# The head of a fused three-layer kernel rewritten: tile loads, moments, weights and 1/sqrt moved between engines

## The reference

```python
x = x + 0.5 * ffn(layernorm(x))
x = x + attn(layernorm(x))        # rope, causal softmax, projection by Wo, bias
x = x + 0.5 * ffn(layernorm(x))
# ffn(h): scores against 128 slots, the 8 highest chosen, softmax over them, their values
# through two small matrices; times a gate; plus h
# gate: sigmoid of a clipped sum of a learned term (gelu MLP) and
#       log1p(var(h)) / mean(log1p(var(h))), the mean over all 2048 rows
# layernorm(x) = (x - mean) / sqrt(var + 1e-5)
```

## Time and profile before

| | us |
|---|---|
| median of three runs | 1456.96 |
| lowest and highest | 1456.8, 1458.84 |
| the profiled execution | 1457.93 |
| its span, first to last instruction | 1456.1 |

### The profile page before, as it was taken

How to read it: one execution, slowest core, us unless ns; L and a number is a source line. 1 busy time by engine, 2 the same in 40 slices (tenths; PEclk the granted TensorE clock), 3 DMA queues, 4 the chain that set the end, 5 groups by cost and what they waited for, 6 DMA issues and landing times.

```text
span 1456.1 us, 26905 instructions
## 1 busy us (share of the span) xinstructions
PE 1370.9 (94%) x8689; PEld 777.2 (53%) x8818; DVE 1137.5 (78%) x2816; ACT 958.9 (66%) x2423; POOL 848.0 (58%) x1343
## 2 busy tenths in 40 slices
PE   5578999998999999999999999999999999999986
PEld 4344555554555655555555655555555555555543
DVE  6787868887788878979778787888777788868655
ACT  4567686776677767666766766666766667666734
POOL 3778778888875454446656455445644565454412
PEclk9799999999999999999999999999999999999998
DMA  9646668778667566556657666557666677555443
GB/s 314 224 90 145 144 154 196 174 178 203 164 157 150 126 142 133 130 123 149 141 129 158 134 125 142 125 129 145 138 139 133 133 151 157 121 142 108 93 76 116
DMA packets 440269, 212.16 MB, mean 146 GB/s; under 512 B 382113, under 2 KB 383329, under 8 KB 440129
## 3 DMA queue, kind: packets, MB, share of 16 engines
q1 hardware_dynamic: 438016, 206.24, 61.5%
q10 hardware_dynamic: 2112, 4.19, 0.9%
HBM read 91.88 MB, written 25.17 MB: 80 GB/s over the span
## 4 chain that ended last, share of the span: by engine, by line
PE 71%; POOL 12%; ACT 7%; DVE 6%; issue 3%; DMA 1%; SPq 0%; DVEq 0%; ACTq 0%
PE PJ L1235 16%; PE PJ L1234 15%; PE PJ L1236 15%; POOL t L562 4%; PE PV L1234 4%; PE PV L1236 4%; PE PV L1235 4%; PE SC L1399 4%; PE SC L1400 4%; PE SC L1398 3%; ACT p L727 2%; POOL wsp L554 2%; POOL qTl L567 2%; POOL wosp L554 1%; POOL oTl L577 1%
## 5 line engine op out<-in xcount | busy, mean ns | idle before, releaser
L577 POOL TENSOR_TENSOR oTl<-of,oTf 128x256 f16<-128x256 f32 x256 | 167.6, 675 | 375.5 <-ACT oTf L719 375.5
L727 ACT ACTIVATE p<-p,mn 128x512 f32<-128x512 f32 (+3 forms) x512 | 280.9, 549 | 86.3 <-DVE mn L1041 86.1
L1051 DVE SCALAR_TENSOR_TENSOR phl<-p,ri,phl 128x128 f16<-128x128 f32 (+3 forms) x512 | 311.1, 647 | 0.0
L562 POOL TENSOR_TENSOR t<-t 128x256 f32<-128x256 f32 x320 | 232.8, 749 | 43.0 <-DVE t L1014 42.4
L738 ACT ACTIVATE phl<-p,ri 128x128 f16<-128x128 f32 (+3 forms) x512 | 245.6, 550 | 4.1
L1234 PE MATMUL PJ<-XT,wsp 128*128 128x512 f16 x640 | 243.4, 380 | 5.0 <-DVE t L1014 3.3
L1235 PE MATMUL PJ<-XT,wsp 128*128 128x512 f16 x640 | 243.1, 380 | 0.0
L1236 PE MATMUL PJ<-XT,wsp 128*128 128x512 f16 x640 | 243.1, 380 | 0.0
L567 POOL TENSOR_TENSOR qTl<-t,qTh 128x256 f16<-128x256 f32 x256 | 169.7, 684 | 93.2 <-ACT qTh L703 93.2
L1041 DVE CUSTOM_DVE_ANT_0 p<-SC,maskw 128x512 f32<-128x512 f32 (+3 forms) x512 | 219.7, 485 | 2.1
L1235 PE MATMUL PJ<-wosp,oTf 128*128 128x512 f16 x512 | 194.0, 379 | 4.4
(11 more groups left out here) (208 smaller groups left out, 2679.1 us busy)
## 6 DMA issues: line engine op xcount, KB each, us to landing
wsp<-kept SPq DMA_DIRECT2D x150, 256.0 KB, 3.1
wosp<-kept SPq DMA_DIRECT2D x96, 256.0 KB, 3.4
raw<-in_wqkv SPq DMA_DIRECT2D x48, 256.0 KB, 4.4
kept<-wsp SPq DMA_DIRECT2D x42, 256.0 KB, 2.5
raw<-in_wo SPq DMA_DIRECT2D x32, 256.0 KB, 4.7
kept<-wosp SPq DMA_DIRECT2D x32, 256.0 KB, 3.1
X<-in_x ACTq DMA_DIRECT2D x4, 1024.0 KB, 11.4
pTf<-phl SPq DMA_TRANSPOSE x256, 3.8
```

Of the source, the lines that this page charges most:

```text
L562: ins = nc.gpsimd.tensor_tensor(t1[:, j, c], t1[:, j, c], t2[:, j, c], ALU.add)
L727: ins = nc.scalar.activation(pt, pt, ACT.Exp, bias=mn[:, par, i:i + 1], scale=-1.0, accum_out=rs[:, par, i:i + 1])
L1051: nc.vector.scalar_tensor_tensor(out=phl[:, par, low(i, 0):low(i, i) + 1, :], in0=p[:, par, SOFF[i]:SOFF[i] + w].rearrange("p (k t) -> p k ...
```

## The change

- Loads. ScalarE's queue issues X's tiles 0, 1 and 2, 3 as two loads, then three small ones (`lrb`, `bu1`, `wu2T`); tiles 4 to 15 are issued by SP, between its other loads. SP no longer waits for tiles 8 to 11 before the weights.
- Moments. VectorE keeps tiles 0 to 9; for tiles 10 to 15 ScalarE sums the differences to the row's first element and their squares (`sums`), and VectorE turns the sums into moments. In the second normalisation the sum comes with the update of `X` (`aux_first`) and the squares from ScalarE (`squares`).
- 1/sqrt. `root` is now Ln and then Exp with scale -0.5, which are in one table set; `ve`, `sd` and the reciprocal go. `gelu` loads its table ahead of its wait and the other set right after.
- GpSimd makes the first base updates of `X` (`x * xa + xb`), the low half `ul`, and both halves of the first four weights. A weight's low half goes in two pieces of 256 columns in place of four of 128, in the loop too.
- The four `W` weights of n = 1 leave the head's list and are made in steps 6 to 8, as for later n.
- V of n = 0 is projected ahead of K, its first three row tiles before K and the last after Q. VectorE does the whole rope of K and the first Q but for the cast. The second `deviation` of k = 0 moves from the head into step 0.
- `penalty` and `minima_ffn` go; `top` marks and takes the minimum for its two tiles with one fused operation per tile, in the loop and the tail too.
- On TensorE the four key matmuls of the setup come first, and `HID` ahead of the `PV` product.

The diff, cut; of the head's written-out lists only the lines that stay or are new are shown, their old form is in the kernel printed above. Three dots also part pieces of different functions.

```diff
+BYACT = 10
+NSPLIT = 4
...
-FIRST = [("K", 0, 0, 0), ("Q", 0, 0, 0), ("V", 0, 0, 0), ("Q", 0, 1, 0)]
+FIRST = [("V", 0, 0, 0), ("K", 0, 0, 0), ("Q", 0, 0, 0), ("Q", 0, 1, 0)]
...
-  + [(1, k) for k in KINDS])
+  + [(1, k) for k in PIECES])
...
+load_x(4, 4)
...
+load_x(8, 4)
+load_x(12, 4)
+for dst, src in ((bu2[:, :], f_bu2.to_broadcast([P, 1])), (gw[:, :], f_gw.to_broadcast([P, 1])),
...
-sp.wait_ge(ld_x[2], 16)
...
+    if r < NSPLIT:
+        pool.wait_ge(ld_r[r], 16)
+        nc.gpsimd.tensor_copy(w[:, 0, :].bitcast(BF16), raw[:, r, :]).then_inc(w_own, 1)
+        pool.wait_ge(w_own, r + 1)
+    else:
+        pool.wait_ge(w_hi, r - NSPLIT + 1)
+    for c in parts(2):
...
-for r in range(6):
+pool.wait_ge(ld_fu, 16)
+pool.wait_ge(fs_hi, 5)
+nc.gpsimd.tensor_tensor(ul[:, :, :], fwu1T, uh[:, :, :], ALU.subtract).then_inc(fs_ul, 1)
+pool.wait_ge(x_ab[0], 1)
+for n in range(4):
+    nc.gpsimd.tensor_scalar(X[:, n, :], X[:, n, :], xa[:, 0, n:n + 1], xb[:, 0, n:n + 1], ALU.mult,
+                            ALU.add).then_inc(x_up[0], 1)
+for r in range(NHEAD):
     weight_low(r)
-penalty(0, 0)
-for r in range(6, NHEAD):
-    weight_low(r)
-for kind, n, idx, _ in FIRST:
-    if kind in "QK":
-        rope(kind, n, idx)
+rope("Q", 0, 1)
...
-for i in range(4):
-    act.dma_start(X[:, 4 * i:4 * i + 4, :], x_v[:, 4 * i:4 * i + 4, :]).then_inc(ld_x[i], 16)
+roots, totals = [0], [0]
+for n in (0, 2):
+    act.dma_start(X[:, n:n + 2, :], x_v[:, n:n + 2, :]).then_inc(ld_x[n], 16)
+for dst, src in ((lrb[:, :], f_lr.to_broadcast([P, NSLOT])), (bu1[:, :], f_bu1), (wu2T[:, :], f_wu2T)):
+    act.dma_start(dst, src).then_inc(ld_fs, 16)
+LOGS = "natural_log_exp_and_others"
...
-    act.wait_ge(ln_v[k], call + 1)
-    nc.scalar.activation(sd[:, k, c0:c1], ve[:, k, c0:c1], ACT.Sqrt).then_inc(ln_sd[k], 1)
+    c = slice(c0, c1)
+    act.wait_ge(ln_v[k], 3 if k == 0 and call else call + 1)
+    nc.scalar.activation(lvar[:, k, c], mv[:, k, c, 1], ACT.Ln, bias=eps[:, 0:1]).then_inc(ln_log, 1)
+    roots[0] += 1
+    act.wait_ge(ln_log, roots[0])
+    nc.scalar.activation(rstd[:, k, c], lvar[:, k, c], ACT.Exp, scale=-0.5).then_inc(ln_sd[k], 1)
...
+def gelu(f, bb, loaded=False):
+    if not loaded:
+        nc.scalar.preload_act_table(ACT.Gelu_apprx_tanh)
...
+    nc.scalar.preload_act_table_set(LOGS)
...
+def total(n, func, sums_):
+    j = totals[0]
+    totals[0] += 1
+    if j >= NROPE:
+        act.wait_ge(a_tot, j - NROPE + 1)
+    nc.scalar.activation(t2[:, j % NROPE, :], X[:, n, :], func, bias=X[:, n, 0:1], scale=-1.0,
+                         accum_out=sums_).then_inc(a_tot, 1)
+def sums(n):
+    act.wait_ge(ld_x[n // 4 * 4], 16)
+    total(n, ACT.Identity, s1[:, 0, n:n + 1])
+    total(n, ACT.Square, s2[:, 0, n:n + 1])
...
+nc.scalar.preload_act_table_set(LOGS)
+act.wait_ge(cst0, 1)
+act.wait_ge(fs_pe, 1)
+nc.scalar.copy(rk[:, :], PJ[0:RDIM, 3, 0:NSLOT]).then_inc(fs_ev, 1)
+act.wait_ge(fs_pe, 2)
+nc.scalar.copy(rmat[:, :], PJ[0:BOT, 2, 0:NSLOT]).then_inc(fs_ev, 1)
+root(0, 0, 0, 4)
 for c in range(CC):
     act.wait_ge(fs_pe, 3 + c)
     nc.scalar.copy(ah[:, c, :], setup_bank(c)).then_inc(fs_hi, 1)
 act.wait_ge(ld_fu, 16)
 nc.scalar.copy(uh[:, :, :], fwu1T).then_inc(fs_hi, 1)
 for i in range(4):
     turned_hi(0, 0, i)
+nc.scalar.preload_act_table(ACT.Gelu_apprx_tanh)
+for n in range(BYACT, BYACT + 2):
+    sums(n)
+act.wait_ge(fs_pe, 7)
+nc.scalar.copy(u1T[:, :], SC[0:VB, 0, 0:NSLOT]).then_inc(fs_ev, 1)
+for n in range(BYACT + 2, NT):
+    sums(n)
+act.wait_ge(ld_fs, 96)
+gelu(0, 0, True)
+exps_ffn(0, 0)
+gate_exp(0, 0, 4)
+logs(0)
 act.wait_ge(fs_pe, 8)
 nc.scalar.copy(v2h[:, :], PV[:, :]).then_inc(fs_hi, 1)
 e_hi(0, 0)
 gate_exp(1, 0, 4)
 for i in range(4):
+    squares(i)
+root(1, 0, 0, 4)
+root(0, 1, 4, NT)
+for r in range(4, 7):
     weight_high(r)
+turned_hi(1, 0, 0)
+turned_hi(1, 0, 1)
+weight_high(7)
+turned_hi(1, 0, 2)
+turned_hi(1, 0, 3)
+for r in range(8, NHEAD):
+    weight_high(r)
+rope("K", 0, 0)
+rope("Q", 0, 0)
+value_hi(0)
+rope("Q", 0, 1)
...
-    link(nc.vector.reciprocal(rstd[:, k, c], sd[:, k, c]))
     link(nc.vector.tensor_tensor(nw[:, k, c], rstd[:, k, c], rstd[:, k, c], ALU.mult))
-    link(nc.vector.tensor_tensor(nw[:, k, c], nw[:, k, c], ve[:, k, c], ALU.mult))
+    link(nc.vector.scalar_tensor_tensor(out=nw[:, k, c], in0=var, scalar=EPS, in1=nw[:, k, c],
+                                        op0=ALU.add, op1=ALU.mult))
...
-    if j == 1:
-        nc.vector.tensor_scalar(mr[:, :, :], mr[:, :, :], 0.99 * SELECTED, MASKED,
-                                ALU.is_gt, ALU.mult).then_inc(r_pen[f], 1)
+    ts = slice(2 * j, 2 * j + 2)
+    link(nc.vector.tensor_scalar(mr[:, ts, :], mr[:, ts, :], 0.99 * SELECTED, MASKED, ALU.is_gt, ALU.mult))
+    for i in (2 * j, 2 * j + 1):
+        n = 4 * bb + i
+        ins = nc.vector.tensor_tensor_reduce(
+            out=asc[:, f, i, :], in0=asc[:, f, i, :], in1=mr[:, i, :], scale=1.0, scalar=3e38,
+            op0=ALU.add, op1=ALU.min, accum_out=mnr[:, f, n:n + 1])
+    ins.then_inc(r_mn[f], 1)
...
+def rope_total(r):
+    dve.wait_ge(rope_mul, r + 1)
+    nc.vector.tensor_tensor(t1[:, r, :], t1[:, r, :], t2[:, r, :], ALU.add).then_inc(rope_sum, 1)
+def rope_low(r, hi, lo):
+    dve.wait_ge(rope_hi, r + 1)
+    nc.vector.tensor_tensor(lo, t1[:, r, :], hi, ALU.subtract).then_inc(rope_lo, 1)
...
+def moments_of_sums():
+    c = slice(BYACT, NT)
+    dve.wait_ge(a_tot, 2 * (NT - BYACT))
+    link(nc.vector.tensor_scalar(s1[:, 0, c], s1[:, 0, c], 1.0 / C, None, ALU.mult))
+    nc.vector.tensor_tensor(mv[:, 0, c, 0], X[:, c, 0], s1[:, 0, c], ALU.subtract)
+    link(nc.vector.tensor_tensor(dm[:, 0, c], s1[:, 0, c], s1[:, 0, c], ALU.mult))
+    nc.vector.scalar_tensor_tensor(out=mv[:, 0, c, 1], in0=s2[:, 0, c], scalar=1.0 / C, in1=dm[:, 0, c],
+                                   op0=ALU.mult, op1=ALU.subtract).then_inc(ln_v[0], 1)
+def aux_first(i):
+    dve.wait_ge(r_aux[0], i + 1)
+    dve.wait_ge(x_up[0], i + 1)
+    dve.wait_ge(r_gs[0], 1)
+    nc.vector.scalar_tensor_tensor(out=X[:, i, :], in0=bank(("AUX", 0, 0, i)), scalar=gs[:, 0, i:i + 1],
+                                   in1=X[:, i, :], op0=ALU.mult, op1=ALU.add,
+                                   accum_out=s1[:, 1, i:i + 1]).then_inc(r_xd[0], 1)
+def variance_of_squares():
+    c = slice(0, 4)
+    dve.wait_ge(r_xd[0], 4)
+    link(nc.vector.tensor_scalar(mv[:, 1, c, 0], s1[:, 1, c], 1.0 / C, None, ALU.mult))
+    link(nc.vector.tensor_tensor(dm[:, 1, c], X[:, c, 0], mv[:, 1, c, 0], ALU.subtract))
+    link(nc.vector.tensor_tensor(dm[:, 1, c], dm[:, 1, c], dm[:, 1, c], ALU.mult))
+    dve.wait_ge(a_tot, 2 * (NT - BYACT) + 4)
+    nc.vector.scalar_tensor_tensor(out=mv[:, 1, c, 1], in0=s2[:, 1, c], scalar=1.0 / C, in1=dm[:, 1, c],
+                                   op0=ALU.mult, op1=ALU.subtract).then_inc(ln_v[1], 1)
...
 for n in range(4):
     arrived(n)
 variance(0, 0, 4)
 deviation(0, 0, 0, 4)
 for i in range(4):
     normal(0, 0, i)
+for c in range(CC):
+    setup_lo(c)
 for i in range(4):
     turned_lo(0, 0, i)
+base_factors(0, 0, 4)
+for n in range(4, 8):
+    arrived(n)
 dve.wait_ge(ld_fs, 96)
 take_scores(0, 0, 0)
 top(0, 0, 0)
+for n in range(8, BYACT):
+    arrived(n)
 take_scores(0, 0, 1)
 top(0, 0, 1)
 learned(0, 0)
 gate_1(0, 0, 4, 1)
+variance(0, 4, BYACT)
+moments_of_sums()
+dve.wait_ge(ln_v[0], 3)
+variance_logs(0)
+log_sum(0)
 dve.wait_ge(fs_hi, 6)
 nc.vector.tensor_tensor(v2l[:, :], PV[:, :], v2h[:, :], ALU.subtract).then_inc(fs_lo, 1)
 e_lo(0, 0)
 log_mean(0)
 gate_2(0, 0, 0, 4)
 gate_3(0, 1, 0, 4)
 scales(0, 0, 4, 1)
 for i in range(4):
+    aux_first(i)
+variance_of_squares()
...
+rope("K", 0, 0)
+rope_total(0)
+rope("Q", 0, 0)
+rope_total(1)
+rope_low(0, kTh[:, 0, :], kTl[:, 0, :])
+rope_low(1, qTh[:, 0, :], qTl[:, 0, :])
+value_lo(0)
+rope("Q", 0, 1)
...
+    if s == 0:
+        deviation(0, 1, 4, NT)
+        base_factors(0, 4, NT)
...
+pe.wait_ge(ld_fq, 16)
+for c in range(CC):
+    mm(setup_bank(c)[:, NSLOT:2 * NSLOT], fwq[:, c * P:(c + 1) * P], fkeyT[:, :], start=True, stop=True)
...
+pe.wait_ge(fs_ul, 1)
+ffn_task(HEAD[6])
 pe.wait_ge(fs_ev, 3)
 mm(PV[:, :], u1T[:, :], fwvuT, start=True, stop=True).then_inc(fs_pe, 1)
-pe.wait_ge(fs_lo, 5)
...
+project_values(0, range(TB - 1))
+project("K", 0, 0)
+project("Q", 0, 0)
+project_values(0, range(TB - 1, TB)).then_inc(s_v, 1)
+project("Q", 0, 1)
```

171 lines of the change are left out of this document (48 added, 123 removed).

## The result

| us | before | after |
|---|---|---|
| median | 1457.03 (4 runs) | 1446.76 (4 runs) |
| lowest and highest | 1456.8, 1458.84 | 1445.04, 1448.45 |
| the profiled execution | 1457.93 | 1448.45 |
| its span | 1456.1 | 1446.6 |

The ratio is 0.9926, with a 95% interval of 0.9914 to 0.9938: 10.3 us faster, where 23 were forecast, and 1.8 above the upper end of the range. In what follows L12 is line 12 of the kernel that the row is from.

What follows compares the result with a forecast made beforehand. TensorE's losses were put down to the head's chain of waits and GpSimd from 80 to 400 us. Head 13.0, loop 8.5 and 0.5, tail 1.0 summed to 23.0, giving 1434 us; range 1424 to 1445.

Steps and rivals of the forecast that it cites:

- The head up to rope K: Loads, moments, gates and second normalisation before the first K's rope: rope K at 51.7 us instead of 64.28.
- K, Q, V: Head, rope K to first minimum: VectorE does all in a row in 9.8 us, first minimum at 61.5, 13.6 earlier.
- The loop: Up to 400 us: GpSimd's shorter weight work gains 8.5 us, bounds 0 and 15, plus 0.5 from 80 to 140.
- slower: Rival, loop: wider GpSimd pieces hold VectorE, 0.26 us for each of 128 pieces, 33 in all, 1476 us; chance 0.03.
- The moved weights: Four weights of n = 1 moved from the head into steps 6 to 8: 5.4 us more of GpSimd's loop time.
- The clock: Head: V begins sooner after the transposes, so some of it runs at the lower clock level, costing 0.6 us.
- The tail: End of the kernel: penalty gone, exponentials 0.8 us earlier, one small saving; gain 1.0 us, bounds 0.5 and 1.3.
- only the head: Rival: the loop gains nothing, through the four moved weights and TensorE waits with other reasons; 1442.5 us, chance 0.20.
- same: Rival, whole kernel: no difference at all, gains and losses cancelling; chance 0.02.

Runs made afterwards that it cites:

- e13: Kernel after, with GpSimd writing zeros three times in place of each loop weight's low-half subtraction (result incomplete): 1436.55 us.
- e5: Kernel after, with GpSimd writing zeros once in place of each loop weight's low-half subtraction (result incomplete): 1424.51 us.
- e4: Kernel after, with the first K's and first Q's rope product written back to PSUM, so VectorE's sum has one operand there: 1443.50 us.
- e3: Kernel after, with GpSimd making the low halves of the head's last four weights only after VectorE's low halves of the first K and Q: 1443.68 us.
- e8: Kernel after, with the first K's and Q's rope product in PSUM and GpSimd's last two head weights behind VectorE's first low halves: 1442.95 us.
- e7: Kernel after, with the four W weights of n = 1 back in the head's list, casts and low halves behind the second Q: 1444.75 us.
- e1: Kernel after, with GpSimd's low halves of the weights back in four pieces of 128 columns: 1449.57 us.
- e6: Kernel after, with two GpSimd casts of the whole weight in place of each loop weight's low-half subtraction (result partly wrong): 1438.28 us.

## Why the prediction was wrong, point by point

**The head up to rope K** held, each point 1.0 to 1.8 late, from the loads on: `fwr` landed at 7.74 (6.7 forecast) and `fwq` at 8.64, and the last `XT` correction ended at 18.75 (17.0). From there the intervals were right. ScalarE's timeline, as the earlier trace rows:

```profile
18.04 1.28 ACT L800 ACT_TABLE_LOAD   x1
...
27.97 0.66 ACT L690 ACTIVATE gT<-PJ,bu 128x512 f32<-128x512 f32 x1
28.65 1.28 ACT L692 ACT_TABLE_LOAD   x1
```

The gelu came 8.65 after the table load's end (12 sums of 0.72 and a copy, 8.9 forecast), `gs` 10.0 after the gelu (10.0), the second normalisation 5.7 after `gs` (5.8), rope K 9.3 after that (9.4). The table load again has no drain ahead of it or behind: that at 18.04 starts 0.02 us after the cast before it, and the first sum starts 0.01 after its end. The trace of before had it so, unlike the Trainium skill (ScalarE: Activation LUTs, What ACT_TABLE_LOAD costs), which adds 1380 ns to every switch. GpSimd's base updates ended at 22.01 (22) and its own weights at 29.99 (32).

**K, Q, V** is the step of the head that failed: "now VectorE does all in a row: three ropes of 2.1, five operations of 0.7 = 9.8". It took 14.05, of which 4.5 are the one sum. The working asked what hides GpSimd's work, and not what GpSimd's work does to the operation that the change moves beside it. The sum had stood on GpSimd itself, in the queue of the pieces, where it could not collide with them. Without the 4.5 the row takes 9.6, so the sum of its own durations was right.

**The loop** (8.5 and 0.5 forecast, a loss of 0.4 measured) failed as the rival *slower* had it in kind. The term priced GpSimd's time and put VectorE's at nothing. GpSimd's time itself was sized well: all pieces in the loop take 118.9 us before and 97.0 after, with four weights more, 22 us less where 24 less 5.4 were forecast. What failed is what it was to buy. The hold was priced only in the rival of 0.03, against which stood "half as many pieces give half as many collisions". Half as many pieces were each longer, and `phl`, four times a step, took 130 ns more in the mean. VectorE was busy 84% of 200 to 400 us in place of 79%, and its 41 us of idle time, the second argument against, did not keep the time out of the chain, where `phl` went from 4.1% to 10.8%. The rival's price was 0.26 for each of 128 pieces, 33 us; `phl` measured some 14 us in all, and even that wasn't all lost. Nor is it shown that GpSimd's time would have bought 8.5 without the hold. e13's 9.9 comes with the hold of the kernel before taken away too. From e13 to e5 GpSimd's writes fall from 100.8 to 33.5 us and the loop gains 10.9, 0.16 for each us; by this estimate the 22 us were worth 3.6. The working also took the mean clock of 0.98 as 4 us at the lower level; at 0.5 against 1 it is 8 us of 200. The moved weights were set at 5.4 of GpSimd's time, and cost 2.8.

The Trainium skill (SBUF — State Buffer, Two separate sides), which the prediction named beside the rival, says that a VectorE instruction with two SBUF operands and a GpSimd instruction that reads SBUF exclude each other for a whole instruction. e4 agrees with the first condition and e13 with the second (`phl` at 612 ns beside writes alone). The kernel after shows more than one instruction's block: the loser lost seven pieces in a row.

**The clock**, 0.6, came as forecast in kind: the granted clock was 0.50 from 46 to 48 and 0.90 from 48 to 50, where V starts at 47.83. No run shows what it cost. But TensorE idled from 58.7 to 64.88, with the stall of 5.18 in it, and the clock fell again, which was in no term:

```profile
60.00:62.00 2.00, 0.00 (x0) 0.00 (x0) 1.97 (x4) 0.62 (x1) 0.00 (x0) 1.00 1.04 402
62.00:64.00 2.00, 0.00 (x0) 0.00 (x0) 1.88 (x4) 0.92 (x2) 0.00 (x0) 0.51 1.06 397
64.00:66.00 2.00, 1.12 (x3) 0.58 (x5) 1.99 (x4) 0.18 (x1) 0.00 (x0) 0.50 0.97 312
```

The stall isn't the only cause: e4, without it, idled from 57.5 to 60.35 and was at 0.60 and 0.54 from 60 to 64. In e3 and e8, which idled 1.5 and 1.7 us there, the clock stayed at 1.00.

**The tail** gave 0.6 of 1.0, within its bounds: `gt` took 0.17 where it had 0.96. The last `gs` takes 1.02 in both kernels (1433.81 after), a hold that stayed.

**The rivals.** The time lies between *only the head* (1442.5) and *same*. *Only the head* had the loop's result, and one of its reasons, the four moved weights (2.8 us, by e7); the other, waits that have nothing to do with GpSimd, fell with e5. The range lacked the case in which the head's and the loop's gain are both cut by the same mechanism.

Open is why VectorE's sum is kept out for a whole queue, or nearly so, in one profile and slips between two pieces in another. In the three with a short sum it began 0.42 to 0.53 us before GpSimd's next piece, in five with a long one 0.19 to 0.24 before; the sixth, e7, began 0.58 before and was long too, so the distance alone does not settle it. It was not varied on purpose. Not split, either, are the 1.9 us that e7 lost in the head, and the loop's gain of the change among its other parts than the pieces and the moved weights.

## What to carry to other kernels

Before an operation is moved from GpSimd to VectorE, or GpSimd's instructions are made wider, list which of VectorE's instructions on the path have both operands in SBUF while GpSimd reads SBUF, and price them at the end of GpSimd's queue, not at their own duration. Add those like `pTf` here, one operand and the result in SBUF, which took half as long again. One operand in PSUM, or a pause on GpSimd until the critical instruction is through, took the stall away (3 us here each; the pause gave 1.5 of its gain up again where the paused work stood ahead of something wanted). When an edit that moved a landing by 2 us moves nothing at the end, compare each later point of the head before calling the edit worthless: a stall may have changed beside it.

## What the runs showed of the hardware

A VectorE sum of 0.69 us took 5.18 beside GpSimd's queued subtractions (8.19 beside narrower ones in e1), and 0.69 beside the same queue with one operand in PSUM (e4). Four normalisations with one tile operand in SBUF took 2.98 beside GpSimd's pieces and 1.92 without. GpSimd's writes of zeros (0.52 us for 512 columns of f16) left `phl` at 612 ns, as without any work there; one-operand casts left it at 823, close to the subtraction's 886 (e6). When the sum did get in (e13, 1.09 us), GpSimd's eight pieces around it took 5.51 in place of 5.06, so the cost then is shared.
